# Where three full-array products stand between the attention heads on TensorE: gate and two expert products moved to the start of a slot

## The reference, cut to what matters

```python
mod = (_silu(L0_c) @ L0_wmod).reshape(L0_c.shape[0], 6, 1, -1)
h = _layernorm(x, axis=-1) * (1 + ca) + sa
x = x + ga * _L0_attn_ref(h, L0_attn_w_qkv, L0_attn_b_qkv, L0_attn_w_out, L0_attn_b_out)
h = _layernorm(x, axis=-1) * (1 + cb) + sb
x = x + gb * _L0_ffn_ref(h, L0_ffn_gate_W, L0_ffn_expert_W, L0_ffn_out_W)
...
# attention, of each head: causal mask with a slope, softmax, times v
scores = jnp.einsum('bhqd,bhkd->bhqk', q, k) / np.sqrt(hd)
scores = scores + _alibi_causal_mask(S, scores.dtype)
probs = jax.nn.softmax(scores, axis=-1)
out = jnp.einsum('bhqk,bhkd->bhqd', probs, v)
...
# mixture: gate, count over a threshold, expert products, output product
p = jax.nn.softmax(jnp.einsum('bsd,ed->bse', x, gate_W), axis=-1).reshape(N, E)
tpi = (p > TOP_P).astype(jnp.int32)
cnt = jnp.sum(tpi[:, :, None] == jnp.arange(E)[None, None, :], axis=1)
scale = cnt.astype(x.dtype) * p
h = jnp.einsum('nd,ehd->neh', x2, expert_W)
final = jnp.einsum('neh,ne->nh', h, scale)
out = jnp.einsum('nh,dh->nd', final, out_W).reshape(B, S, D)
```

## Time and profile before

| what | us |
|---|---|
| median of 3 runs | 1579.26 |
| lowest and highest run | 1576.92, 1581.57 |
| the profiled execution's own time | 1575.65 |
| its span, first to last instruction | 1573.7 |
| mean granted TensorE clock, share of full speed | 0.981 |
| PE busy | 1470.1 (93%) |
| DVE busy | 1268.1 (81%) |
| ACT busy | 1147.5 (73%) |
| POOL busy | 868.4 (55%) |

### The profile page before, as it was taken

One profiled execution on the slowest core, in us unless ns is written; L12 is line 12 of the kernel. 1 busy time (PEld: TensorE's weight loads), 2 busy tenths in 40 slices (PEclk: granted clock), 3 DMA queues, 4 the chain that ended last, 5 costly groups with the idle time before them and its releaser, 6 DMA issues.

```text
span 1573.7 us, 56191 instructions
## 1 busy us (share of the span) xinstructions
PE 1470.1 (93%) x21460; PEld 943.8 (60%) x21460; DVE 1268.1 (81%) x3017; ACT 1147.5 (73%) x2466; POOL 868.4 (55%) x935
## 2 busy tenths in 40 slices
PE   6898999999999999999999999999999999999974
PEld 5555666666666566666666666665666666566542
DVE  6777888888888888888888888888888888888722
ACT  1477777777777877777787777778777777777651
POOL 2125556556655655665565566556556655655555
PEclk9799999999999999999999999999999999999987
DMA  5344555555455555545555554555555455554420
GB/s 169 98 150 127 167 169 159 178 151 166 142 165 172 156 178 154 165 139 170 171 154 178 151 164 141 169 171 156 174 155 167 138 167 172 156 178 138 145 80 31
DMA packets 197762, 241.07 MB, mean 153 GB/s; under 512 B 22286, under 2 KB 147670, under 8 KB 197494
## 3 DMA queue, kind: packets, MB, share of 16 engines
q1 hardware_dynamic: 197500, 237.48, 49.9%
HBM read 135.06 MB, written 101.81 MB: 151 GB/s over the span
## 4 chain that ended last, share of the span: by engine, by line
PE 60%; DMA 11%; DVE 10%; issue 7%; SPq 6%; POOL 3%; ACT 2%; POOLq 0%; DVEq 0%; ACTq 0%
PE ps L522 25%; PE ps L657 11%; PE ps L652 7%; DMA qk_d<-qk_st 6%; PE ps L711 6%; PE ps L706 4%; DVE mxp L940 3%; DMA kz<-qk_d 3%; PE ps L672 2%; SPq L380 2%; PE ps L568 2%; DVE zr L952 1%; DVE ve_c L865 1%; SPq L396 1%; DVE st_c L851 1%
## 5 line engine op out<-in xcount | busy, mean ns | idle before, releaser
L940 DVE TENSOR_REDUCE mxp<-ps 128x4 f32<-128x512 f32 (+1 forms) x1536 | 842.2, 592 | 156.7 <-PE ps L672 151.7
L749 ACT ACTIVATE prob<-ps 128x512 f32<-128x512 f32 (+1 forms) x1536 | 732.0, 525 | 119.3 <-PE ps L657 113.4
L657 PE MATMUL ps<-qs,kz 50*128 50x128 f16 (+2 forms) x3584 | 405.8, 240 | 12.7 <-DVE mxp L940 10.5
L672 PE MATMUL ps<-kz,qs 49*128 49x128 f16 (+1 forms) x4096 | 410.6, 231 | 0.1
L657 PEld LDWEIGHTS ps<-qs,kz 50*128 50x128 f16 x3584 | 261.2, 94 | 88.8 <-ACT prob L749 30.3
L672 PEld LDWEIGHTS ps<-kz,qs 49*128 49x128 f16 x4096 | 285.9, 95 | 3.7 <-DVE mxp L940 1.8
L1107 POOL TENSOR_TENSOR om<-oc,rz 128x512 f32<-128x512 f32 x64 | 79.9, 1269 | 332.8 <-DMA rz<-rz_d 332.8
L711 PE MATMUL ps<-prob,va 128*32 128x384 f32 (+2 forms) x3072 | 237.0, 380 | 0.0
L652 PE MATMUL ps<-mk 64*128 64x256 bf16 x1024 | 198.5, 274 | 34.4 <-DMA kz<-qk_d 14.5
L706 PE MATMUL ps<-prob,va 128*32 128x128 f32 x4096 | 209.2, 276 | 0.6 <-DVE qk_st L872 0.6
L668 PE MATMUL ps<-mk 64*128 64x256 bf16 x1024 | 200.8, 276 | 5.5 <-DVE mxp L940 3.1
(11 more groups left out here) (124 smaller groups left out, 2852.7 us busy)
## 6 DMA issues: line engine op xcount, KB each, us to landing
qk_d<-qk_st SPq DMA_DIRECT2D x128, 256.0 KB, 2.9
ou_d<-ou SPq DMA_DIRECT2D x128, 256.0 KB, 2.3
qs<-qk_d SPq DMA_DIRECT2D x256, 96.0 KB, 2.4
kz<-qk_d SPq DMA_DIRECT2D x256, 96.0 KB, 2.4
xa<-in_L_attn_x SPq DMA_DIRECT2D x32, 512.0 KB, 5.4
qk_d<-qk_st SPq DMA_DIRECT2D x128, 128.0 KB, 3.5
xc<-in_L_attn_x SPq DMA_DIRECT2D x32, 512.0 KB, 4.4
oc<-ou_d SPq DMA_DIRECT2D x32, 512.0 KB, 5.0
```

The source lines that it names most:

```text
L657: x_ = mm(bank[:, col:col + w * P], kz[rows, h // 2, kt * P:(kt + 1) * P], qs[rows, h // 2, qt * P:(qt + w) * P], start=(n > 0), stop=(n > ...
L672: x_ = mm(bank[:, col * P:(col + w) * P], qs[rows, h // 2, qt * P:(qt + 1) * P], kz[rows, h // 2, kt * P:(kt + w) * P], start=(n > 0), sto ...
L749: nc.scalar.activation(prob[:, h % 8, at:at + w], ps[:, ST + n, 0:w], ACT.Exp, scale=1.0 / FS).then_inc(s["exp_done"], 1)
L940: v.tensor_reduce(mxp[:, g % 2, at, first:first + apart * (BLOCKS[n] - 1) + 1:apart], bank.rearrange("p (m k) -> p m k", k=P), AX.X, ALU.m ...
```

## The change

Three entries of `PE_AT` move. `gate` goes from slot 6, ahead of chunk 2, to slot 7, ahead of `pv` 0. `moe` 1 goes from behind the head of slot 9 to ahead of it, directly behind `qk` 3. `moe` 2 goes from behind the head of slot 11 to ahead of it, directly behind `pv` 1. The two setup steps that stand in place of `gate` 0 and `moe` 2 in iteration 0 (`gate_rows`, `bias_row`) move with them. The tables of the other engines, all waits and all shapes stay.

```diff
     4: [(0, "qk", 0, 1), (0, "qk", 1, 1), (1, "t2", 0, -2)],
     5: [(1, "t2", 1, -2), (1, "v", 0, 1)],
-    6: [(0, "mt", 2, 0), (2, "gate", 0, -2)],
-    7: [(0, "pv", 0, 0), (3, "qk", 2, 1), (3, "moe", 0, -2)],
+    6: [(0, "mt", 2, 0)],
+    7: [(0, "gate", 0, -2), (0, "pv", 0, 0), (3, "qk", 2, 1), (3, "moe", 0, -2)],
     8: [(3, "mt", 3, 0)],
-    9: [(0, "qk", 3, 1), (3, "moe", 1, -2)],
+    9: [(0, "qk", 3, 1), (0, "moe", 1, -2)],
     10: [],
-    11: [(0, "pv", 1, 0), (3, "moe", 2, -2)],
+    11: [(0, "pv", 1, 0), (0, "moe", 2, -2)],
     12: [],
```

## The result

The changed kernel takes 1637.87 us (median of 4 runs, 1636.81 to 1642.5) against 1578.37 us before (4 runs, 1576.92 to 1581.57): a ratio of 1.038, 95% interval 1.0354 to 1.0406, 59.5 us slower. The prediction said 1638. The profiled execution of the changed kernel is the slowest of its four, 1642.5 us.

The account below looks back on a forecast made before the run. PE was taken to pace the batch, DVE not far below. 1575.65 us plus 59.5 (29 iterations) plus 1 (iteration 31) is 1636.1, or 1639.8 on the median's scale; 1638 was said, range 1630 to 1646, wider 1618 to 1652.

Parts of the forecast that it names:

- What bounds the stretch: Slots 9 to 12: PE makes a head in 0.88 us, DVE reads it in 1.62, one PSUM bank per chunk.
- The sum: From `mt` 3 to `moe` 3: 12.32 or 12.22 us instead of 10.25, taken as 2.05 more in 29 iterations.
- The term left open, `pv` to `moe`: `pv` 1 to `moe` 2: 2.31 us, or 2.21 if that transition is free; no row showed it.
- the wait for `negm` 3: At `moe` 1, which needs `negm` 3 from ACT: costs nothing, or some hundredths of a us after the release.
- The gate: Slots 6 and 7: chunk 2 loses its cover, `pv` 0 comes 0.01 to 0.09 us later; counted as nothing.
- (a): Heads run on without a wait, only entries and exits count: 9 to 17 us faster; chance 0.04.
- (c): Only the first pair, slots 9 and 10, costs; the second is milder: about 1606 to 1614 us; chance 0.05.
- (d): More exposed: `moe` 2 waits for `zs` 1 or later slots lose cover, 0.3 to 0.5 a batch, 1648 to 1655; chance 0.05.
- (b): The wait at the head of slot 8 shrinks and gives part back: 1624 us, at most 1594; chance 0.07.
- follows the products of slot 4: Head of slot 8 waits 0.56 us for a load of queries and keys, whose store follows slot 4's products.

Follow-up runs that it names:

- the faster readers: Exponentials over half the columns from batch 1, row maxima over 64 of each 128: kernel before 1558.7 us (0.985), changed kernel 1588.06 us (1.0057).
- The run with the smaller wait at slot 8: Kernel before with `load_c` and `store_rz` moved behind the stores of `qk` 0 and 1, and `gate` moved as in the change: 1563.16 us, ratio 0.9885.

## Why the prediction was right, step by step

**What bounds the stretch.** Right. The second head of each pair comes 1.53 behind the first, with 0.58 idle for L940, `pv` 1 waits 0.28 for L872, all as iteration 1 had it. The runs of the single moves show that each pair pays by itself, and the faster readers that the reading is what half of it pays for; that the other half is the single bank follows from the distances and was not tested by a kernel with a second one.

**The sum.** 12.32 or 12.22 us was forecast from `mt` 3 to `moe` 3; it is 12.30. The term left open, `pv` to `moe`, took 2.30: that change of kinds costs what `pv` to a head did, so `moe` 2 spares one entry and no exit. `moe` 1 came 1.41 behind `mt` 3, so the wait for `negm` 3 costs nothing that can be seen. 29 times 2.05 was 59.5; the trace has 59.7. The difference of the medians is 59.5.

**What the sum left out.** Outside these stretches the profiled execution is another 7 us longer, of which 1 was forecast. Some 3.5 lie in and behind iteration 31, of which 2.3 are its own stretch from `mt` 3 to `moe` 3, where 1 was estimated. About 1.3 lie ahead of iteration 2, where "under 1" was said; the moved setup step is not shown as their cause, for with `moe` 1 moved alone, where `gate_rows` stays, iteration 2 starts 2.2 us later than before. The other 2.2 lie in iterations 2 to 30, 1.5 of them at the heads of slot 8, whose wait varies from 0 to 1.7 us between iterations of one run. The median is 4.6 us below that execution, so part of this belongs to that one execution. The forecast's own terms added up to 1639.8 on the scale of the medians, and 1638 was said without a reason for the difference. That it agrees with the median to a tenth of a microsecond is luck; the 2.05 us a batch is not.

**The gate.** The step was right: the entry and the exit it would spare are taken by chunk 2, which must wait for the exponentials of slot 5 and had been hidden by the gate. The loss is about 0.01 us a batch, the low end of 0.01 to 0.09. The run with the smaller wait at slot 8 shows that the second half of the argument, that this wait swallows whatever the gate does, was not needed.

**The rivals.** (a), no waits, is excluded by the pair of 0.58 idle times, (c) by the two single moves, (d) by `moe` 2: in iteration 14 `zs` 1 ended at 753.08 and `moe` 2 started at 753.53. (b), that slot 8 gives something back, is excluded by the traces: `moe` 0 to the head of slot 8 has a mean of 2.15 us after and 2.10 before.

**Where a step was wrong.** What the prediction said of slot 8, that the wait there "follows the products of slot 4", was too simple. It follows them only through a DMA list in which two entries wait for other engines first. The runs on the DMA list showed it, and the chain of waits alone had misled.

## What to carry to other kernels

Work that stands between two producers of the same bank is the time in which the reader empties the bank: before grouping it to spare a change between kinds of products (0.1 us each way here), compare the maker's time for a unit with its reader's, and count the banks. Where a stage is missing in the first or last iterations of a pipeline, the trace already contains the experiment, so read the same slots there. In an ordered DMA list, entries that wait for a far engine belong behind those that the bottleneck waits for, all of them at once: here moving one of two brought nothing, moving both brought 18 us, and the other one alone was not tried.

## What the runs showed of the hardware

Not all changes between kinds of products cost the same. From `pv`, whose products fill 32 columns of the array each, to full-array products (`pv` 1 to `moe` 2) costs what `pv` to a head did, 2.30 us against 2.31 from the start of `pv`; the last eight products of `pv` 1 take 0.34 us to the next kind in both, where eight such products before others of `pv` take 0.22. A `mt` of 16 columns followed by the full-array products of `qk` 3 costs nothing that can be seen: 0.11 us from its start to theirs, as far apart as the transposes of 128 columns in `ta` 1 are from each other. The Trainium skill (TensorEngine Tiling (Array Packing), Key Properties) has a rule for the first: a change of tiling mode makes the engine drain first. The traces agree, with about 0.1 us for each change. They show no such price between `mt` and full-array products; whether that is a change of mode at all, no row shows.

Halving the columns of a row maximum over 512 columns took it from a mean of 0.68 to 0.42 us, not to half, which is one reason why readers of half the work did not bring the two heads together.
